# Spreading the routing weights of the first layer's experts: two fp32r parts in 16 rows instead of three bfloat16 parts in 24 rows

## The reference, cut to what matters

```
x1 = x + silu(conv(x))
logits = einsum('bsd,ed->bse', x1, router_w) + router_b
top_v, top_i = top_k(logits, 2);  top_w = softmax(top_v)
rw = sum(one_hot(top_i, 8) * top_w[..., None], axis=-2)
ye = silu(einsum('bsd,eod->bseo', x1, expert_w) + expert_b)
combined = einsum('bse,bseo->bso', rw, ye)
moe_out = einsum('bsd,od->bso', combined, out_w) + out_b
```

## Time and profile before

| what | value |
|---|---|
| median of 3 runs | 6018.69 us (6008.41 to 6022.03) |
| span of the profiled execution | 6018.3 us |
| mean granted TensorE clock | 0.927 of 2.4 GHz |
| PE / PEld busy | 5016.6 us (83%) / 2504.4 us (42%) |
| DVE / POOL / ACT busy | 4198.7 / 3312.4 / 3106.3 us |
| first experts' stage, first to last expert product | about 2027 to 2203 us |
| second | about 2747 to 2922 us |

### The profile page before, as it was taken

How to read it: one execution, slowest core, us unless ns; L and a number is a source line. 1 busy time by engine, 2 the same in 40 slices (tenths; PEclk the granted TensorE clock), 3 DMA queues, 4 the chain that set the end, 5 groups by cost and what they waited for, 6 DMA issues and landing times. The chain is left out here.

```text
span 6018.3 us, 79139 instructions
## 1 busy us (share of the span) xinstructions
PE 5016.6 (83%) x22359; PEld 2504.4 (42%) x22446; DVE 4198.7 (70%) x6070; ACT 3106.3 (52%) x5312; POOL 3312.4 (55%) x2371
## 2 busy tenths in 40 slices
PE   5888888888887888978887999855996899963997
PEld 1333333333332433434343455433664344432664
DVE  5999999999997563056575878643775566652775
ACT  4666666666664454235554777621332577821332
POOL 3888988898885353034443444345343555536333
PEclk8999999999999899989988999966998899976998
DMA  2234322222221002000003333111553443311455
GB/s 79 86 136 152 115 89 89 82 92 89 89 82 39 0 0 85 0 0 0 6 5 79 88 85 93 35 48 66 188 189 107 101 95 97 75 38 51 169 188 175
DMA packets 203028, 494.17 MB, mean 82 GB/s; under 512 B 32432, under 2 KB 57520, under 8 KB 191280
## 3 DMA queue, kind: packets, MB, share of 16 engines
q1 hardware_dynamic: 183536, 451.33, 24.3%
q0 software_dynamic: 18176, 37.79, 1.8%
q10 hardware_dynamic: 960, 0.79, 0.1%
HBM read 381.65 MB, written 108.12 MB: 81 GB/s over the span
## 5 line engine op out<-in xcount | busy, mean ns | idle before, releaser
L396 POOL TENSOR_TENSOR mamba_bu<-mamba_du,mamba_b_all 128x1024 f32<-128x1024 f32 x512 | 1199.4, 2360 | 184.2 <-PE psum L490 168.6
L667 DVE TENSOR_TENSOR_SCAN mamba_bu<-psum,mamba_bu 128x512 f32<-128x512 f32 x1024 | 1190.2, 1207 | 68.9 <-ACT psum L599 34.4
L490 PE MATMUL psum<-mamba_bu,consts 128*128 128x512 f32 x2048 | 965.8, 594 | 8.2 <-issue 5.1
L599 ACT ACTIVATE psum<-mamba_delta,A 128x510 f32<-128x510 f32 x1024 | 682.9, 683 | 386.9 <-DVE mamba_bu L667 373.7
L1646 POOL DMA_INDIRECT results<-ffn_moe_y_rows,ffn_moe_row_of x312 | 303.0, 971 | 507.2 <-DVE ffn_moe_y_rows L1836 426.2
L1761 ACT ACTIVATE ffn_moe_act<-ffn_moe_act 128x512 f32<-128x512 f32 x344 | 217.0, 631 | 688.9 <-DVE ffn_moe_act L1805 484.5
L673 DVE TENSOR_TENSOR mamba_bu<-mamba_bu,psum 128x1024 f32<-128x1024 f32 x448 | 537.3, 1199 | 4.9 <-remote 1.8
L490 PEld LDWEIGHTS psum<-mamba_bu,consts 128*128 128x128 f32 x2048 | 392.7, 192 | 346.1 <-issue 327.8
L2201 POOL TENSOR_TENSOR loc_q_bd<-loc_q_max,weights_l1a 128x512 fp32r<-128x512 f32 x256 | 275.0, 1103 | 379.3 <-DVE loc_q_max L2456 370.7
L2201 POOL TENSOR_TENSOR cau_q_bd<-cau_q_max,weights_l1b 128x512 fp32r<-128x512 f32 x256 | 258.5, 1042 | 243.6 <-DVE cau_q_max L2456 178.1
L2447 DVE TENSOR_REDUCE cau_top<-psum 128x2 f32<-128x512 f32 (+1 forms) x384 | 263.2, 692 | 183.0 <-PE psum L2271 169.2
(11 more groups left out here) (415 smaller groups left out, 11141.9 us busy)
## 6 DMA issues: line engine op xcount, KB each, us to landing
mamba_b_all<-b_rows SPq DMA_DIRECT2D x256, 512.0 KB
ffn_moe_w_gu<-gate_up_parts SPq DMA_DIRECT2D x78, 1024.0 KB
pairs<-empty_rows SPq DMA_DIRECT2D x6, 3432.0 KB, 13.1
ffn_moe_got<-pairs SPq DMA_DIRECT2D x78, 264.0 KB, 3.3
ffn_moe_w_down<-in_l_moe SPq DMA_DIRECT2D x78, 256.0 KB
mamba_c_rows<-b_rows SPq DMA_DIRECT2D x32, 512.0 KB
qk_rows<-loc_qk SPq DMA_DIRECT2D x16, 1024.0 KB, 9.2
ffn_moe_back<-results SPq DMA_DIRECT2D x32, 512.0 KB, 4.7
```

Source lines behind the costliest of these rows:

```text
L396: nc.gpsimd.tensor_tensor(bu[:, J % BU, :, :], du[:, q % 2, :, :], b, ALU.mult).then_inc(bu_ready, 1)
L490: last = nc.tensor.matmul(ysum[:, h, :], mem.ident, bu[:, J % BU, h, :], start=False, stop=(n == NST - 1), skip_group_check=True)
L599: nc.scalar.activation(by_seq(dA[i % DECAYS])[:, :, 1:S], by_seq(delta[:, q % 2, h, :])[:, :, 1:S], ACT.Exp, scale=mem.A[:, q % 2, h * NST ...
L667: nc.vector.tensor_tensor_scan(bu[:, J % BU, h, :], dA[i % DECAYS], bu[:, J % BU, h, :], 0.0, ALU.mult, ALU.add).then_inc(scanned, 1)
```

## The change

The weights are split into two fp32r parts (high, and what is left) instead of three bfloat16 parts. `parts`, `tile_parts` and `rows` become fp32r; the parts take 16 rows instead of 24. The identity of `turn` and the 0/1 matrix of `spread` are needed in the same format, so `l0_weights` makes fp32r copies of both. The split on DVE has two instructions instead of four, and the tensor `rest` goes. The number and the order of the products on PE, and all waits in the loop, stay. The sizes that the built program gives to the array stay too: `spread` uses 32 rows by 128 columns of it, `turn` 128 rows by 32 columns, in both kernels.

```diff
@@ l0_weights
+            nc.vector.tensor_copy(mem.ident_r[:, :], mem.ident)
+            nc.vector.tensor_copy(mem.one_hot_r[:, :], mem.one_hot[:, 0:NE])
             nc.vector.tensor_copy(mem.expert_high[:, :], w["experts"]).then_inc(rounded, 1)
@@ split_comb
     nc.vector.tensor_copy(parts[:, :, 0:NE], comb).then_inc(split, 1)
     dve.wait_ge(split, 1 + LEAD)
-    nc.vector.tensor_tensor(rest, comb, parts[:, :, 0:NE], ALU.subtract).then_inc(split, 1)
-    dve.wait_ge(split, 2 + LEAD)
-    nc.vector.tensor_copy(parts[:, :, NE:2 * NE], rest).then_inc(split, 1)
-    dve.wait_ge(split, 3 + LEAD)
-    nc.vector.tensor_tensor(parts[:, :, 2 * NE:3 * NE], rest, parts[:, :, NE:2 * NE], ALU.subtract).then_inc(split, 1)
+    nc.vector.tensor_tensor(parts[:, :, NE:2 * NE], comb, parts[:, :, 0:NE], ALU.subtract).then_inc(split, 1)
@@ l0_experts
-        rest = sb("rest", NB, NE)
-        parts = sb("parts", NB, 3 * NE, dt=BF16)
-        tile_parts = sb("tile_parts", SUB, 3 * NE, dt=BF16)
-        rows = sb("rows", 2, T, dt=BF16)
+        ROWS = 2 * NE
+        parts = sb("parts", NB, ROWS, dt=F32R)
+        tile_parts = sb("tile_parts", SUB, ROWS, dt=F32R)
+        rows = sb("rows", 2, T, dt=F32R)
@@ turn
-                    last = nc.tensor.matmul(mem.bank[6][0:3 * NE, j * 128:(j + 1) * 128], tile_parts[:, j, :], mem.ident16, start=True, stop=True)
+                    last = nc.tensor.matmul(mem.bank[6][0:ROWS, j * 128:(j + 1) * 128], tile_parts[:, j, :], mem.ident_r[:, :], start=True, stop=True)
@@ spread
-                nc.tensor.matmul(mem.bank[2 + e % 2], mem.one_hot[0:3 * NE, e:e + 1].to_broadcast([3 * NE, 128]), rows[0:3 * NE, s, :],
+                nc.tensor.matmul(mem.bank[2 + e % 2], mem.one_hot_r[0:ROWS, e:e + 1].to_broadcast([ROWS, 128]), rows[0:ROWS, s, :],
                                  start=True, stop=True).then_inc(spread_ready, 1)
@@ take_rows
-                nc.scalar.activation(rows[0:3 * NE, s, :], mem.bank[6][0:3 * NE, :], ACT.Identity).then_inc(rows_ready, 1)
+                nc.scalar.activation(rows[0:ROWS, s, :], mem.bank[6][0:ROWS, :], ACT.Identity).then_inc(rows_ready, 1)
```

More of the change, by code:

```diff
@@ L895, in _, with split_comb @@
             take_logits(NT - 1, 1)
-def split_comb(nc, dve, comb, rest, parts, split):
+def split_comb(nc, dve, comb, parts, split):
     nc.vector.tensor_copy(parts[:, :, 0:NE], comb).then_inc(split, 1)
     dve.wait_ge(split, 1 + LEAD)
-    nc.vector.tensor_tensor(rest, comb, parts[:, :, 0:NE], ALU.subtract).then_inc(split, 1)
-    dve.wait_ge(split, 2 + LEAD)
-    nc.vector.tensor_copy(parts[:, :, NE:2 * NE], rest).then_inc(split, 1)
-    dve.wait_ge(split, 3 + LEAD)
-    nc.vector.tensor_tensor(parts[:, :, 2 * NE:3 * NE], rest, parts[:, :, NE:2 * NE], ALU.subtract).then_inc(split, 1)
+    nc.vector.tensor_tensor(parts[:, :, NE:2 * NE], comb, parts[:, :, 0:NE], ALU.subtract).then_inc(split, 1)
 def tiles_with_next(eng, step):
@@ L960, in tile @@
                         x_low(t + 1, 1 - s)
-            pool.wait_ge(split, 4 + LEAD)
+            pool.wait_ge(split, 2 + LEAD)
             copy_parts(0)
@@ L1071, in tile @@
                         finish(t - 1, 1 - s)
-            split_comb(nc, dve, comb[:, :, :], rest[:, :, :], parts, split)
+            split_comb(nc, dve, comb[:, :, :], parts, split)
             tiles_with_next(dve, tile)
@@ L3096, in program @@
             mem.expert_high = held_l0.enter_context(nc.sbuf_tensor("expert_high", [D, NE * D], F32R))
+            mem.ident_r = held_l0.enter_context(nc.sbuf_tensor("ident_r", [D, D], F32R))
+            mem.one_hot_r = held_l0.enter_context(nc.sbuf_tensor("one_hot_r", [D, NE], F32R))
             mem.expert_low = held_l0.enter_context(nc.sbuf_tensor("expert_low", [D, NE * D], F32R))
```

## The result

The changed kernel takes 6237.68 us, the median of 4 runs (6173.61 to 6305.65), against 6017.77 us before. The ratio is 1.0255 with a 95% interval of 1.0231 to 1.0279. The four runs fall into two groups, 6174 and 6175 us and 6300 and 6306 us, and the interval takes the first; the profile is one of 6175 us (span 6172.8). I had forecast 6043 us.

What follows compares the result with a forecast made beforehand. PE, busy throughout each tile, was taken to bound the experts' stage. Spread +26.7, turn 0, split -2.4 and preparation +0.2 summed to +24.5 us on 6018.3, so 6043 us; range 6020 to 6066.

Steps and rivals of the forecast that it cites:

- What bounds the stage: Experts' stage: PE sets the tile time, busy 10.84 of 10.84 us, in each of 32 tiles.
- The spread's exposed load, +0.10 us each: 256 spread products: the exposed weight load becomes fp32r, +0.10 us each; 26.7 us in all with the half-clock part.
- The estimate of 0.08 us: Estimate from the Trainium skill page for the spread's load: 0.08 us more per spread, 20.5 us instead of 25.6.
- The emptying around a narrow product: Spread: a product using few array rows empties the array before and after, about 0.10 us each; loads cannot run ahead.
- Rival 2: Spread: an fp32r product takes all rows, so the emptying goes; DVE bounds at about 9.3 us, total about 5967; chance 0.12.
- The turn, net 0: 32 turns of four products: +0.22 us for fp32r, -0.22 for no emptying and a load running ahead.
- the nearest row: Four fp32 transposes of the last layer, 0.43 us, taken as the time of the turn's four fp32r products.
- my low end of 0.22: Turn at one column per cycle, 0.21 us for its four products: -0.22 us per turn, -7.0 us in all.
- Rival 1: The turn runs at plain fp32's rate, +13.8 to +20.8 us: total 6057 to 6064 us; chance 0.25.
- Split and preparation: DVE's shorter split saves 1.2 us at each of two stage starts; two preparation copies add about 0.2 us once.
- rival 4: Clock: second stage also starts with 29.7 us at 1.2 GHz, 6058 us, or the first does not, 6028; chance 0.05.

Runs made afterwards that it cites:

- experiment 1: Kernel before with only the spread product in fp32r; 24 rows, three bfloat16 parts and bfloat16 turn stay: 6069.22 us against 6026.87, ratio 1.0081.
- experiment 2: Changed kernel with rows stored as bfloat16 and spread by the bfloat16 0/1 matrix; two-part split and fp32r turn stay: 6020.21 us, ratio 0.9985.
- experiment 4: Changed kernel with the spread over all 128 rows, those above 16 zero: 5989.11 us against 6026.87, ratio 0.9941.
- experiment 3: Kernel before with the bfloat16 spread over all 128 rows, those above 24 zero: 5996.5 us against 6026.87, ratio 0.9953.
- experiment 8: Changed kernel with filler products keeping PE busy before each experts' stage, loop untouched: 6026.07 us against 6023.03, ratio 1.0004.
- experiment 11: Changed kernel with two idle vector instructions, 1.4 us, ahead of the split at each stage's start: 6055.05 us against 6024.57, ratio 1.0045.
- experiment 9: Changed kernel with one more small product per tile, before the spread of expert 2, into an unused bank: 6122.38 us against 6024.57, ratio 1.0165.
- experiment 6: Changed kernel with bfloat16 parts and bfloat16 turn; 16 rows and fp32r spread stay: 6124.94 us against 6023.03, ratio 1.016.
- experiment 10: Changed kernel with one idle vector instruction, 0.7 us, ahead of the split at each stage's start: median 6242.07 us, against 6024.57.
- experiment 5: Changed kernel run again without any edit, five runs: median 6296.55 us against 6023.03, ratio 1.0449.

## Why the prediction was wrong

- *What bounds the stage:* right. PE is busy throughout, before and after.
- *The spread's exposed load, +0.10 us each:* right. The interval went from 0.31 to 0.42, and experiment 1 shows it in the spread alone. It is not bound to the number of rows: 16 bfloat16 rows cost what 24 do (experiment 2), and over 128 rows the same fp32r load hides (experiment 4). The estimate of 0.08 us beside it took the bfloat16 load for four times as fast as the fp32r one; the profiles have 91 and 181 ns.
- *The emptying around a narrow product:* supported; experiments 3 and 4 remove the extra time and the late load together by using all rows. There, however, I took DVE's busy time for the bound (9.0 to 9.4 us a tile) and measured 10.30: DVE waits for ScalarE and GpSimd between its instructions. Rival 2, sized in the same way, would have given back too much. How the extra splits into emptying and load, no run measured by itself.
- *The turn, net 0:* mis-sized. The four products went from 0.32 to 0.25 us, where the nearest row had made me add 0.22, and the product behind them from 0.34 to 0.28, not to 0.23. It gives back 0.13 us a tile, a little over half of my low end of 0.22. Rival 1 is out.
- *Split and preparation:* right, -1.2 us a stage and +0.2 us.
- The sum of these, 32 x 0.71 - 2.4 + 0.2 = +20.5 us, was forecast as 24.5. Two kernels check the 22.7 us of the loop, with 0.43 us lost for each us at half clock. The two stages before take 360.2 us, of which 34 at half, so 345.4 at full clock. Those of experiment 8 take 368.4, all but 1 us at full clock, some 23 more. Those of experiment 11 take 397.1, of which 69 at half, so 367.2, some 22 more. Experiment 8 comes out level with the kernel before as a whole because it also wins back the 15 us that half clock costs there.
- *The step that failed* is the clock, which the forecast held at what it was before: it has no term for a longer stay at half clock. Only rival 4 moved it: "If the second stage did likewise, 6058 us". I took the 29.7 us at half clock as a fixed piece at the head of a stage, which could occur once more or not, and gave it 0.05. (Its 14.8 us was too much even so: by my own factor of 1.75 it is 12.7.) It is not a piece of fixed length. A stage starts low where PE idles before it; then the clock rises soon, or stays low tile after tile. In the changed kernel it stays low in one or in both stages. The first stage so took 139 us more than before (324.5 against 185.5, of which 11 are the loop's own price), and the second takes 126 us more when it stays low too (324.5 against 198.7).
- *Shown:* the low clock at the stage's start is the cause of the loss (8: the same loop, held high, costs only its own price). *Supported by few runs:* timing, and not the amount of work, decides when the clock rises (11: a later start, the loop untouched, four runs; 9: a tile longer by 0.2 us that does more and rises sooner). *Argued only:* that the changed loop can rise only at the stretch of project, first product and turn, and that its tile of 20.45 us keeps meeting the chip at the same wrong place. For it speaks that with the narrow fp32r spread all ten rises in the profiles came 4.0 to 4.6 us behind a project's start (experiments 1, 6, 9 and 11, and the second stages of the changed kernel and of experiment 10); and that tiles of 20.63 and 20.66 us rose behind the third to seventh project, where those of 20.45 rose behind the first or not at all. No experiment moved the project inside the tile, and why the first sessions of the changed kernel differ (in two of the first four runs only one stage stayed low, in the next five always both) stays open.

## What to carry to other kernels

Where a loop keeps TensorE busy but starts at half clock after an idle stretch, read how long it stays there as a risk of the whole loop, not as a constant: here 0.2 us in a tile of 20.45 or 1.4 us ahead of the loop switched it, and comparing two kernels then compares that switch. Keep TensorE busy up to the loop's first product, with filler products if need be; it made the price of this change visible again. And look for a product with few rows among full ones. An expert's four products took 1.21 us with a bfloat16 spread of 24 rows, 1.31 with the fp32r one of 16, and 0.93 over all rows filled up with zeros, which gave 28 and 36 us.

## What was not expected of the hardware

- The same loop, 100% busy, stayed at 1.2 GHz for 324.5 us or held 2.4 GHz for 183 us, by the state it started in (experiments 5 and 8).
- Adding a product to each tile made the kernel 50 to 180 us faster than the changed one's runs, and starting the stage 1.4 us later 120 to 250 us (experiments 9 and 11).
- Four fp32r products of 128 columns took 0.25 us against 0.32 in bfloat16, so fp32r is as fast at 128 columns. The load of the full product behind them ran ahead although they have only 16 weight columns; behind the fp32r spread with 16 rows it did not.
